# Four banks of plain scores as one set of two banks and two single banks, in the shared attention of a transformer kernel

## The reference

```
x = x + L2_xattn(layernorm(x), ctx, ctx)      # and L3 alike
QH, KVH, D = 32, 8, 16                        # 4 query heads share one key/value head
scores  = einsum('bkgsd,bktd->bkgst', q, k) / sqrt(D)
weights = softmax(scores)                     # over t, 512 keys
out     = einsum('bkgst,bktd->bkgsd', weights, v)     # k = v = ctx
```

## Time and profile before

| | before |
|---|---|
| median of 3 runs | 4300.75 us (4295.9 to 4312.59) |
| the profiled execution | 4315.3 us, its span 4312.5 us |
| mean granted TensorE clock, share of full | 0.834 |
| PE busy | 3586.3 us, 83% |
| DVE busy | 2323.3 us, 54% |
| ACT busy | 1901.2 us, 44% |
| L1639, maxima, x512 | 612.1 us, 1220 ns each |
| L1621, exponentials, x1024 | 549.3 us, 599 ns each |
| L1559 and L1543, score products, x1024 each | 530.9 and 549.6 us |
| L1572, results, x2048 | 414.6 us |

### The profile page before, as it was taken

How to read it: one execution, slowest core, us unless ns; L and a number is a source line. 1 busy time by engine, 2 the same in 40 slices (tenths; PEclk the granted TensorE clock), 3 DMA queues, 4 the chain that set the end, 5 groups by cost and what they waited for, 6 DMA issues and landing times. The chain is left out here.

```text
span 4312.5 us, 61624 instructions
## 1 busy us (share of the span) xinstructions
PE 3586.3 (83%) x16914; PEld 2348.5 (54%) x16918; DVE 2323.3 (54%) x3739; ACT 1901.2 (44%) x3267; POOL 607.8 (14%) x901
## 2 busy tenths in 40 slices
PE   3369997999737996588888699998987888888998
PEld 2147775666525885233333377887762333325886
DVE  6954454555342334655555445665566555545665
ACT  5643323555213543344444433665334444444343
POOL 2410003544211001200000130221110000000000
PEclk7679998999858998567676699999996767658999
DMA  4434441300013333411110253676433111101223
GB/s 139 144 107 138 138 133 67 130 0 0 23 60 122 105 112 108 149 36 33 32 35 24 77 191 106 233 245 211 137 102 116 32 35 32 32 19 56 95 94 113
DMA packets 191369, 405.49 MB, mean 94 GB/s; under 512 B 45892, under 2 KB 46020, under 8 KB 190578
## 3 DMA queue, kind: packets, MB, share of 16 engines
q1 hardware_dynamic: 157906, 287.52, 21.2%
q0 software_dynamic: 22480, 96.23, 6.6%
q10 hardware_dynamic: 10864, 20.45, 1.3%
HBM read 313.37 MB, written 88.08 MB: 93 GB/s over the span
## 5 line engine op out<-in xcount | busy, mean ns | idle before, releaser
L1639 DVE TENSOR_REDUCE at_maxima<-psum 128x2 f32<-128x1024 f32 x512 | 612.1, 1220 | 500.5 <-PE psum L1543 499.4
L1621 ACT ACTIVATE at_probs<-psum 128x512 f32<-128x512 f32 x1024 | 549.3, 599 | 608.6 <-PE psum L1559 603.4
L1559 PE MATMUL psum<-at_qT,at_kT 50*128 50x512 f32 x1024 | 530.9, 621 | 167.2 <-DVE at_result L1660 120.3
L1559 PEld LDWEIGHTS psum<-at_qT,at_kT 50*128 50x128 f32 x1024 | 234.2, 262 | 675.7 <-issue 399.6
L1543 PE MATMUL psum<-at_kT,at_qT 48*128 48x512 f32 x1024 | 549.6, 635 | 18.4 <-DVE at_maxima L1639 14.7
L1572 PE MATMUL psum<-at_probs,at_vals 128*32 128x512 f32 x2048 | 414.6, 892 | 0.0
L573 PE MATMUL psum<-f_xT_hi,ffn_w_hi 128*128 x1024 | 405.8, 396 | 10.2 <-DVE ffn_w_lo L486 2.6
L573 PE MATMUL psum<-f_xT_lo,ffn_w_hi 128*128 x1024 | 405.6, 396 | 0.0
L1543 PEld LDWEIGHTS psum<-at_kT,at_qT 48*128 48x128 f32 x1024 | 231.1, 259 | 94.8 <-DVE at_maxima L1639 89.4
L590 PE MATMUL psum<-ffn_w_hi,ffn_hid_hi 128*128 128x512 f32 x768 | 269.4, 391 | 1.3 <-ACT ffn_hid_hi L636 1.3
L387 PE MATMUL psum<-ident,n_normed 128*128 128x128 f32 x448 | 93.5, 380 | 196.7 <-ACT n_normed L353 157.7
(11 more groups left out here) (396 smaller groups left out, 7279.3 us busy)
## 6 DMA issues: line engine op xcount, KB each, us to landing
ffn_w_raw<-in_stream SPq DMA_DIRECT2D x262, 256.0 KB, 2.8
ffn_w_hi<-quantized SPq DMA_DIRECT2D x66, 512.0 KB, 3.5
ffn_w_hi<-quantized SPq DMA_DIRECT2D x65, 256.0 KB
at_qT<-q_hi SPq DMA_DIRECT2D x256, 64.0 KB, 2.2
ffn2a_w_raw<-in_shared2a SPq DMA_DIRECT2D x26, 512.0 KB, 3.6
ffn2b_w_raw<-in_shared2b SPq DMA_DIRECT2D x26, 512.0 KB, 3.6
qz_raw<-in_stream SPq DMA_DIRECT2D x17, 768.0 KB, 4.2
quantized<-qz_quant POOLq DMA_DIRECT2D x16, 768.0 KB, 3.5
```

The source lines that it names most:

```text
L1559: pe.matmul(scoreT[turn_of(n)][:, :], kT[r][half(h % 2, USED + 2), t * P:(t + 1) * P], qT[r][half(h % 2, USED + 2), h // 2, :], start=True ...
L1621: act.activation(probs[n % RING][:, :], scoreT[turn_of(n)][:, :], ACT.Exp, scale=factor).then_inc(exped, 1)
L1639: dve.tensor_reduce(maxima[:, 2 * jj:2 * jj + 2, t], score[m % 2].rearrange("p (h s) -> p h s", h=2), AX.X, ALU.max).then_inc(maxed, 1)
```

## The change

The four banks of plain scores become three sets in turn: banks 0 and 1 together, bank 2, bank 3. A group has 12 sets, `SETS` = (0, 2), (2, 1), (3, 1), (4, 2), ..., each with its first product and its number of banks, and so 12 maxima, four over 1024 columns and eight over 512. `maxed` begins at 3, and a set waits for the third maximum before it. `LAST`, `VALUES` and `MOVE` go up by one. `finish` is done behind the maximum of the set that holds product 7, and no longer behind that of products 8 and 9.

```diff
--- before.py
+++ after.py
@@ -1389,13 +1389,13 @@
     USED = PARTS * HD
     HALF = P // 2
     PAIRS = H * TB
-    SETS = PAIRS // 2
+    SETS = [(n, 2 if n % 4 == 0 else 1) for n in range(PAIRS) if n % 4 != 1]
     RING, SLOTS = 2 * H, 4
     OW = P // H
     ROUND = GROUPS // B
     ROUNDS = (GROUPS - 1 - SLOTS) // ROUND
     LOADS, PUTS = 2 * PARTS * 2, H
-    LAST, VALUES, MOVE, RES = 2, (6, 10, 14), 2, 7
+    LAST, VALUES, MOVE, RES = 3, (7, 11, 15), 3, 7
     TURNS = 3
     with stage_room(k) as room:
         ctx, block = room.memory, room.block
@@ -1413,7 +1413,7 @@
         split = sb("split", [P, H, 2, TB], F32R)
         across = [sb(f"across{r}", [P, 2 * H * TB]) for r in range(2)]
         result = sb("result", [P, TB, H * HD])
-        score, scoreT, res = [room.psum[:, 1024 * m:1024 * m + 1024] for m in range(2)], room.banks[4:4 + TURNS], room.banks[7]
+        score, scoreT, res = room.banks[0:4], room.banks[4:4 + TURNS], room.banks[7]
         turn = room.tiles(4 + (RES + 1) % TURNS)
         landed, put = ([k.sems(ctx, nm, f"{n}{r}")[0] for r in range(SLOTS)] for n in ("landed", "put"))
         (cleared, consts, spilled, scored, maxed, max_split, max_turned, max_out, scoredT, exped, valued, vals_kept, res_moved, turned_res,
@@ -1448,6 +1448,10 @@
 
         def half(par, count):
             return slice(HALF * par, HALF * par + count)
+
+        def set_of(n):
+
+            return sum(first <= n for first, _ in SETS) - 1
 
         def turn_of(n):
 
@@ -1535,14 +1539,14 @@
             def scores(g, place, j, n):
 
                 jj, par, t = head_tile(n)
-                r, m = place % SLOTS, n // 2
+                r = place % SLOTS
                 if n == 0:
                     pe.wait_ge(landed[r], LOADS * DMA * (use(place, j) + 1))
-                if n % 2 == 0:
-                    pe.wait_ge(maxed, SETS * g + m + 1)
-                mm = pe.matmul(score[m % 2][:, 512 * (n % 2):512 * (n % 2) + S], qT[r][half(par, USED), jj, t * P:(t + 1) * P],
-                               kT[r][half(par, USED), :], start=True, stop=True)
-                if n % 2 == 1:
+                if n % 4 != 1:
+                    pe.wait_ge(maxed, len(SETS) * g + set_of(n) + 1)
+                mm = pe.matmul(score[n % 4][:, :], qT[r][half(par, USED), jj, t * P:(t + 1) * P], kT[r][half(par, USED), :],
+                               start=True, stop=True)
+                if n % 4 != 0:
                     mm.then_inc(scored, 1)
 
             def scores_T(g, place, j, n):
@@ -1628,19 +1632,22 @@
 
         @block.vector
         def _(dve):
-            dve.sem_inc(maxed, 2)
+            dve.sem_inc(maxed, 3)
             dve.sem_inc(added, 1)
             dve.sem_inc(finished, 1)
             dve.wait_ge(consts, 4)
 
             def max_set(g, m):
-                jj, _, t = head_tile(2 * m)
-                dve.wait_ge(scored, SETS * g + m + 1)
-                dve.tensor_reduce(maxima[:, 2 * jj:2 * jj + 2, t], score[m % 2].rearrange("p (h s) -> p h s", h=2), AX.X, ALU.max).then_inc(maxed, 1)
+                n, banks = SETS[m]
+                jj, par, t = head_tile(n)
+                h = 2 * jj + 1 - par
+                dve.wait_ge(scored, len(SETS) * g + m + 1)
+                scores = room.psum[:, 512 * (n % 4):512 * (n % 4 + banks)].rearrange("p (h s) -> p h s", h=banks)
+                dve.tensor_reduce(maxima[:, h:h + banks, t], scores, AX.X, ALU.max).then_inc(maxed, 1)
 
             def split_maxima(g, place):
                 hi, lo = split[:, :, 0, :], split[:, :, 1, :]
-                dve.wait_ge(maxed, 2 + SETS * (g + 1))
+                dve.wait_ge(maxed, 3 + len(SETS) * (g + 1))
                 if not (isinstance(g, int) and g < 1):
                     dve.wait_ge(max_turned, g)
                 dve.tensor_copy(hi, maxima[:, :, :]).then_inc(max_split, 1)
@@ -1660,19 +1667,19 @@
                 dve.tensor_tensor(result[:, :, :].rearrange("p t (h d) -> p t h d", h=H), r[:, :, :, 0:HD],
                                   inv[:, :, :].rearrange("p t (h o) -> p t h o", o=1).to_broadcast([P, TB, H, HD]), ALU.mult).then_inc(finished, 1)
 
-            for m in range(SETS):
+            for m in range(len(SETS)):
                 max_set(0, m)
             split_maxima(0, 0)
-            for m in range(SETS):
+            for m in range(len(SETS)):
                 max_set(1, m)
 
             def slot(s, place, j, ahead):
                 if ahead >= 1:
                     split_maxima(s + 1, place + 1)
-                for m in range(SETS):
+                for m in range(len(SETS)):
                     if ahead >= 2:
                         max_set(s + 2, m)
-                    if m == (RES + 1) // 2 and not is_first(s):
+                    if m == set_of(RES) and not is_first(s):
                         finish(s - 1)
 
             all_slots(dve, slot)
```

## The result

The changed kernel takes 3864.65 us (median of 4 runs, 3861.65 to 3868.05) against 4298.32 us before; the ratio is 0.8997, with a 95% interval of 0.8954 to 0.904. The profiled execution has a span of 3865.0 us. The sum was too small in both cases, and the part on why says where. Times of different sets of runs are therefore compared by their ratio to the kernel before in the same set: 4316.71 us for e1 to e4, 4320.78 for e5 to e8, 4297.78 for e9 and e10.

What follows compares the result with a forecast made beforehand. PE's queue in layers 2 and 3 was taken as the bound, held by waits and a falling clock. 28 slots x (18.9 - 12.0) x 2 layers, with smaller terms, gave 387 us: 4300.75 - 387 = 3914 us, range 3870 to 4075.

Steps and rivals of the forecast that it cites:

- The sum: Whole kernel: 28 slots x (18.9 - 12.0) x 2 layers = 388 us, with smaller terms 389, rounded down to 387 saved.
- All three causes: PE in layers 2 and 3: 2.1 us wait for `finish` at n=10, bank waits at n=6 and 14, falling clock.
- the bank wait's end: Two-bank waits at n=0, 4, 8, 12 covered by two pairs and results, more than a maximum's 1.2 us.
- rival 1: Layers 2 and 3: the clock keeps falling once in two slots; slot 14.7 us, kernel 4065 us; chance 0.17.
- rival 3: DVE becomes the bound by single maxima; at 1.7 us each, kernel 4350 us; chance 0.06 with anything else slower.
- the sum of 11.0: DVE per slot: maxima 9.4 us, split 0.7, `finish` 0.9, together 11.0 us, at most 11.7.
- The clock's way up: Start of layers 2 and 3: two slots each until 2.4 GHz, 17.4 + 14.7 us, costing 16 us in all.
- The number of slots: 28 slots a layer with plain scores, from the first `finish`, used to multiply the saving per slot.
- The last two slots: End of each layer, without plain scores: some 14 us shorter if the clock stays up, counted as 7 per layer.
- The slot: One group of 16 products in layers 2 and 3: 18.9 us before, 12.0 after.
- PE's sum: A slot at 2.4 GHz on PE: four groups of 2.6, 3.4, 2.75 and 2.6 us, 11.4 in all, the lower bound.
- SP's chain: SP's send, twelve loads, puts and landing: 12.0 to 12.5 us before n=0 of the next slot may start.

Runs made afterwards that it cites:

- e1: The kernel before with only `finish` moved early, behind the maximum of products 6 and 7: 4026.36 us, ratio 0.932.
- e4: The kernel before with early `finish` and results moved, sets of two banks kept: 3878.74 us, ratio 0.8994.
- e5: The kernel after with `finish` late again, behind the maximum of products 8 and 9: 4076.79 us, ratio 0.9436.
- e8: The kernel before with early `finish` and results moved, two-bank sets kept, rerun on one chip with e7: 3892.88 us, ratio 0.9017.
- e9: The kernel after with every maximum reading only the first 256 columns of each bank: 3855.62 us, ratio 0.897.
- e10: The kernel after with two more small loads per group in SP's queue ahead of the puts: 3905.14 us, ratio 0.9075.
- F: The part that moves `finish` early; alone on the kernel before, it is e1: 4026.36 us, ratio 0.932.
- e6: The kernel after with LAST, VALUES and MOVE as before (results not moved): 3914.12 us, ratio 0.9062.
- R: The part that moves the results by LAST, VALUES and MOVE; alone on the kernel before: 4081.08 us, ratio 0.9447.
- S: The part with the three new sets; alone, with results and `finish` placed as in the kernel before: 4113.31 us, ratio 0.9488.
- e7: The unaltered kernel after, rerun with six runs on the same chip as e8: 3880.81 us, ratio 0.9011.
- e2: The kernel before with only LAST, VALUES and MOVE moved up by one, late `finish` kept: 4081.08 us, ratio 0.9447.

## Why the prediction was right, and why its range was not

*What holds PE up.* All three causes are shown: the wait for `finish` by F, the bank waits by the rows under e6, the clock by e5. Ratios side by side: F 0.932, R 0.9447, S 0.9488; S and R 0.9436, S and F 0.9062, F and R 0.8994, all 0.8997. The early `finish` is in every version at 0.932 or below. Of the other two parts the moved results are enough; the sets alone leave 33 us (3914 for e6, 3881 for e7). Both cure the same bank wait, and by the prediction's working the results also cover the exp for n=1. The prediction gave the bank wait's end to the change as a whole; that the new sets are not needed for it was in its own working ("stand two pairs and these results") and not drawn.

*The clock.* All kernels with the late `finish` have a clock of 0.68 to 0.86 in the stretches of the two layers, all with the early one 0.94 to 1.00. In the kernel before, the granted clock falls 41 times in the two stretches, and each fall lies between 0.02 us ahead of product 10, the end of the wait for `finish`, and 1.6 us behind it. One more part failed, rival 1's silent assumption that with the wait the clock stays as it was: R or S alone, with the wait at its full 2.1 us, lift it to 0.80 and more. They don't make it fall less often: R alone has 42 falls in the two stretches. But the clock is at 1.2 GHz for 333 us there, and for 703 in the kernel before, so that it comes back up after some 8 us on the mean in place of 16. That this is because PE's work between two waits has fewer gaps is my reading; no run tried it by itself. Rival 1's price (a slot of 14.7 us, 4065 us) is near e5 (14.8 and 15.5 us, 4077 us), but by luck: it took a slot at the high clock as 12.0 us, where e5 has 13.4 with the wait in it, and the high clock for 38% of the time, where e5 has 73% in layer 2 and 61% in layer 3.

In the kernel after the clock falls four times in the two stretches. The first of these is in the timeline of PE; the puts of that slot were issued from 1832.68 on, for 2.56 us (timeline of SP):

```profile
1834.00 1.07 PE L1576 MATMUL psum<-at_probs,at_vals 128*32 128x512 f32 x8
1836.62 0.49 PE L1563 MATMUL psum<-at_qT,at_kT 50*128 50x512 f32 x1 [1.55 <-DMA at_qT<-tops]
...
1837.16 0.84 PE L1563 MATMUL psum<-at_qT,at_kT 50*128 50x512 f32 x2
```

```profile
1824.78 0.35 SPq L1499 DMA_DIRECT2D tops<-at_across  x1
...
1828.72 1.61 SPq L1491 DMA_DIRECT2D at_qT<-q_lo  x1
...
1832.68 2.56 SPq L1510 DMA_DIRECT2D at_qT<-tops  x4
```

One load took 1.61 us to issue where others take 0.37; so the puts came late, PE waited 1.55 us, and worked at 1.2 GHz behind it. What made that issue slow was not tried.

The other three falls have another cause: PE waits 1.56, 0.96 and 0.85 us for ACT's exp of product 0. They are in slots 9 and 17 of layer 2 and 17 of layer 3, the first slots of a pass of the loop in `all_slots`, which has eight slots in a pass. The exp of product 0 starts 1.4 to 1.9 us behind its product in slots 9 and 17, and 0.5 us behind it in nearly all others. Slot 9 of layer 2, in the timelines of PE and of ACT (its product 0 started at 1908.33):

```profile
1910.87 0.49 PE L1563 MATMUL psum<-at_qT,at_kT 50*128 50x512 f32 x1 [1.56 <-ACT at_probs L1625]
```

```profile
1910.22 2.06 ACT L1625 ACTIVATE at_probs<-psum 128x512 f32<-128x512 f32 x4 [1.98 <-PE psum L1563]
```

These three slots took 15.2, 13.5 and 14.9 us. The same two slots are late in the kernel before too (the exp 2.9 to 3.1 us behind product 0, against 0.7), so the change did not bring this. Not every wait of this length is followed by a fall: the longest two of slots 1 to 29 of layer 3, 1.5 us for an exp and 1.4 for the puts, were not. What ACT does there was not tried; the loop is where to look next.

*DVE.* 681 ns was within the bounds, rival 3 is far off. DVE is busy 10.8 us in a slot of 11.9, as the sum of 11.0 had it, and e9 shows that it is not the bound.

*The step that failed: the sum of the saving, in four of its terms.* The cause and the waits were right; 387 us came out where the two layers of the profiled execution gave 446 (414 in slots 1 to 29, 28 in the last two slots, 4 in slot 0).

- The clock's way up, 16 us against: I charged two slots a layer. It was up 1.7 us into slot 1 in layer 2 and 1.3 us before slot 1 in layer 3 (slots 0 and 1 took 14.7 + 11.9 and 13.6 + 13.3 us, not 17.4 + 14.7), and what falls remain are in the mean of 11.9 already. So the charge should have been nothing: 16 us.
- The number of slots: I counted 28 a layer, and there are 29 between the starts of slot 1 and slot 30; the stretch that I called the last two slots began at product 11 of slot 29. That is 7 us a layer: 14 us.
- The last two slots: 14 us a layer, taken at even chances as 7. The clock stayed up in them, and they gave 13.3 and 14.4: 14 us.
- The slot: 19.0 us before, cut rightly, and not 18.9; 11.9 after, and not 12.0. 0.2 x 58 = 12 us.

Together 56 of the 59 us. By the medians the miss is 47 us, since the profiled execution of the kernel before was 14.5 us slower than the median.

That the 12.0 us came so near 11.9 is partly luck. PE's sum was 11.4, and slots without disturbance take 11.54. I lifted it to 12.0 for SP's chain, with a landing of 2.2 us taken from a 64 KB load, which no run shows for the puts: their issue ended at 1835.24, and product 0 began at 1836.62, 1.4 us later. SP's chain is covered in most slots, and what lifts the mean to 11.9 is the few waits above and the falls of the clock behind them, which the 12.0 did not have in it. The range's low end lay 44 us under the forecast, 34 of them for a slot of 11.4 us; none of the first three terms was in it.

## What to carry to other kernels

When PE waits once a period for a short step of another engine, look at what stands ahead of that step in the other engine's queue, and count the clock into its price: here 1.9 us more of waiting a slot cost 2.9 to 3.7. Before buffers are cut finer, look whether work that needs no buffer can be put where the wait is; here one line of constants did all that could be told, and the new sets were not needed. When a period gets shorter, lay every chain beside it, the DMA queue's too: three of them lie within 0.7 us of each other now (PE 11.5 us, SP 11.3 by the estimate under e10, DVE 10.8). DVE alone made faster gave 0.1 us a slot (e9); I expect that a larger gain needs all three, which no run tried.

## What the runs showed of the hardware

Two queued maxima of 512 columns start 0.60 us apart at 681 ns each. With one wait of PE of 2.1 us a slot the granted clock fell 41 times in 58 slots, each time at the end of that wait or up to 1.6 us behind it; in the kernel after, four waits of 0.85 to 1.56 us were followed by one each, and others of 1.4 and 1.5 us by none. The granted clock in the same stretch went from 0.68 to 0.80 by a move of work alone, with the longest wait of PE unchanged at 2.1 us (e2): it fell as often and came back up in half the time. On SP one DMA issue took 1.61 us where its like take 0.37, and in a schedule with 0.2 us of slack PE's wait behind it was followed by a fall of its clock.
